# Where attention outputs are turned: from a turn of their own in a ring of banks to the bank of the turned row maxima

## The reference, cut to what matters

```python
xn = layernorm(x)                                   # x: 4 x 512 x 256
q, k, v = xn @ Wq.T, xn @ Wk.T, xn @ Wv.T           # 4 query groups share 8 heads of k and v, 8 wide
scores = einsum('bsqhd,bthd->bqhst', q, k) / sqrt(8)
a_dot  = einsum('bqhst,bthd->bsqhd', softmax(scores), v)
a_mem  = (elu(q) @ memory) / (elu(q) @ memory_norm)
attn   = a_dot * (1 - w) + a_mem * w                # w = sigmoid(memory_weight)
out    = x + attn + moe(xn)                         # 8 experts, top 2, and a shared expert
```

## Time and profile before

| what | value |
|---|---|
| median of 3 runs | 738.71 us (737.17 to 740.52) |
| profiled execution | 736.45 us, of which the span of the instructions is 734.4 us |
| granted TensorE clock, mean | 1.000 |
| busy share of the span | PE 97%, DVE 80%, ACT 67%, POOL 19% |

### The profile page before, as it was taken

How to read it: one execution, slowest core, us unless ns; L and a number is a source line. 1 busy time by engine, 2 the same in 40 slices (tenths; PEclk the granted TensorE clock), 3 DMA queues, 4 the chain that set the end, 5 groups by cost and what they waited for, 6 DMA issues and landing times.

```text
span 734.4 us, 16848 instructions
## 1 busy us (share of the span) xinstructions
PE 712.1 (97%) x5018; PEld 393.1 (54%) x5019; DVE 589.8 (80%) x1040; ACT 490.0 (67%) x886; POOL 137.7 (19%) x298
## 2 busy tenths in 40 slices
PE   8999999899999999999999999899999999999998
PEld 3455544632222222222222223588888888888887
DVE  6276489899999999999999992577777878766755
ACT  2473600299999999999999898756566665656322
POOL 1000000566642222111222211100000000005750
PEclk9999999999999999999999999999999999999999
DMA  9829200168521111001111362051111111122431
GB/s 304 286 71 325 66 1 0 34 204 258 171 64 33 33 34 34 26 25 33 33 33 33 97 223 84 15 172 43 57 50 50 50 50 57 43 101 80 137 109 42
DMA packets 50003, 65.42 MB, mean 89 GB/s; under 512 B 8216, under 2 KB 42928, under 8 KB 49968
## 3 DMA queue, kind: packets, MB, share of 16 engines
q1 hardware_dynamic: 37232, 39.92, 17.2%
q10 hardware_dynamic: 9664, 16.66, 6.9%
q0 software_dynamic: 3072, 8.39, 3.6%
HBM read 40.15 MB, written 24.38 MB: 88 GB/s over the span
## 4 chain that ended last, share of the span: by engine, by line
PE 71%; DVE 12%; issue 8%; ACT 7%; DVEq 1%; POOL 1%; ACTq 1%; POOLq 0%
PE ps L1432 14%; DVE smax L1026 10%; PE ps L1500 9%; PE ps L1401 9%; PE ps L1280 7%; PE ps L1456 7%; PE ps L1534 6%; ACT att L752 5%; PE ps L1272 4%; PE ps L1549 3%; PE ps L1304 3%; PE ps L1491 2%; PE ps L1238 2%; ACT o_sb L711 1%; PE ps L1386 1%
## 5 line engine op out<-in xcount | busy, mean ns | idle before, releaser
L1026 DVE TENSOR_REDUCE smax<-ps 128x1 f32<-128x512 f32 x512 | 309.3, 675 | 8.6 <-PE ps L1304 8.6
L752 ACT ACTIVATE att<-ps 128x512 f32<-128x512 f32 x512 | 273.5, 597 | 34.0 <-PE ps L1456 27.9
L1401 PE MATMUL ps<-att,v_head 128*32 128x256 f32 x2048 | 163.4, 391 | 6.3 <-ACT o_sb L711 5.8
L1456 PE MATMUL ps<-att 51*128 51x512 bf16 x512 | 159.8, 383 | 3.4 <-ACT att L752 1.1
L1304 PE MATMUL ps<-att 48*128 48x512 bf16 x512 | 159.0, 384 | 0.0
L1432 PE MATMUL ps<-att_r 128*128 128x512 f32 x456 | 117.6, 407 | 3.2 <-DVE att_r L1087 3.2
L1083 DVE TENSOR_TENSOR att_r<-big,att_r 128x1024 fp32r<-128x1024 f32 x76 | 89.8, 1222 | 24.7 <-ACT att_r L732 24.6
L1456 PEld LDWEIGHTS ps<-att 51*128 51x128 bf16 x512 | 38.3, 93 | 113.9 <-DVE smax L1026 64.5
L1432 PEld LDWEIGHTS ps<-att_r 128*128 128x128 f32 x456 | 85.6, 188 | 21.8 <-DVE att_r L1087 3.8
L1401 PEld LDWEIGHTS ps<-att,v_head 128*32 128x32 f32 x2048 | 40.6, 108 | 92.5 <-issue 49.3
L732 ACT ACTIVATE att_r<-big 128x1024 fp32r x74 | 74.3, 1052 | 19.4 <-issue 19.3
(11 more groups left out here) (167 smaller groups left out, 702.0 us busy)
## 6 DMA issues: line engine op xcount, KB each, us to landing
big<-w ACTq DMA_DIRECT2D x8, 1024.0 KB
q_stacks<-big SPq DMA_DIRECT2D x12, 512.0 KB
att<-q_stacks SPq DMA_DIRECT2D x64, 96.0 KB
slot_x<-zeros SPq DMA_DIRECT2D x1, 4992.0 KB, 17.9
e_x<-slot_x SPq DMA_DIRECT2D x39, 128.0 KB, 2.0
slot_y<-xn SPq DMA_DIRECT2D x39, 128.0 KB, 1.7
big<-w ACTq DMA_DIRECT2D x8, 512.0 KB
att<-k_stacks SPq DMA_DIRECT2D x64, 48.0 KB
```

Source lines behind the costliest of these rows:

```text
L752: act.activation(probs[:, t % 2, g, :], ps[:, RING[turn_of(u) % 3], :], ACT.Exp, scale=SCALE)\
L1026: dve.reduce_max(smax[:, s % 2, 8 * half + v:8 * half + v + 1], ps[:, bank + half, :], X_AXIS)\
L1401: last = pe.matmul(ps[32 * g:32 * (g + 1), 6, queries], v_head[:, s % 2, t, :], probs[:, t % 2, g, queries], start=s % 2 == 0 and t == 0 a ...
L1456: pe.matmul(ps[:, RING[turn % 3], :], k_st[s][rows, P * t:P * (t + 1)], q_st[s][rows, g, :], start=True, stop=True).then_inc(scores_ready, 1)
```

## The change

Outputs have no turn of their own any more: `turn_of` skips turn 6 alone, the sixteen scores use turns 0 to 5 and 7 to 16, and turn 17 stays empty (`NO_TURN`), so that a step still has 18. The outputs of a pair are now turned in the odd step (the second head) behind the pair, after round 2, just ahead of the turned maxima and in the same bank: maxima in columns 0 to 127, outputs in columns 128 to 415. The transposes become four plain fp32 matmuls of the output against `held`, the 4 by 18 columns of the identity that pick out what is needed. `copy_oT` stands on ScalarE between `negate_max` and exponential 6 of the odd step; `finish_o` stands ahead of the maxima of round 5 of the odd step; `add_o` follows in the next even step. Turn 9 (score 8) waits for both readers of the bank.

```diff
-        TURNS, MAX_AT, OUT_AT = 18, 6, 13
+        TURNS, MAX_AT, NO_TURN = 18, 6, 17
+        OUT_COLS = 2 * (DH + 1)
...
-            return u + (u >= MAX_AT) + (u >= OUT_AT - 1)
+            return u + (u >= MAX_AT)
...
-                    if s == 1 and not first:
-                        add_o(blk * 2 - 1, 1, b if h0 == 4 else b - 1, (h0 - 2) % H)
-                    if s == 3:
-                        add_o(blk * 2, 0, b, h0)
+                    if s % 2 == 0 and not first:
+                        add_o(blk * 2 + (s // 2 - 2), s // 2, b if h0 == 4 else b - 1, (h0 + s - 4) % H)
...
+            add_o(PAIRS - 2, 0, BATCH - 1, H - 4)
             add_o(PAIRS - 1, 1, BATCH - 1, H - 2)
...
-                act.activation(oT_sb[:, a, :, :].rearrange("p (w two) n -> p w (two n)", two=2),
-                               ps[:, bank, :].rearrange("p (w n) -> p w n", n=32)[:, :, 0:2 * (DH + 1)],
-                               ACT.Copy).then_inc(oT_copied, 1)
+                act.activation(oT_sb[:, a, :, :].rearrange("p w n -> p (w n)"),
+                               ps[:, bank, P:P + ST * G * OUT_COLS], ACT.Copy).then_inc(oT_copied, 1)
...
-                    if s % 2 == 0 and not first:
-                        if u == 4:
-                            evacuate_o(blk * 2 + (s // 2 - 1), (s // 2 + 1) % 2)
-                        if u == 12:
-                            copy_oT(blk * 2 + (s // 2 - 1), (s // 2 + 1) % 2)
+                    if u == MAX_AT and s % 2 == 1 and not first:
+                        copy_oT(blk * 2 + (s // 2 - 1), (s // 2 + 1) % 2)
+                    if u == 4 and s % 2 == 0 and not first:
+                        evacuate_o(blk * 2 + (s // 2 - 1), (s // 2 + 1) % 2)
...
-                    if v == 7 and s % 2 == 0 and not first:
+                    if v == 5 and s % 2 == 1 and not first:
                         finish_o(blk * 2 + (s // 2 - 1), (s // 2 + 1) % 2)
...
+                if back == NO_TURN:
+                    return
                 if back == MAX_AT:
-                    wait(pe, negm_ready, i + 2)
-                elif back == OUT_AT:
                     wait(pe, oT_copied, outputs)
+                    if not last:
+                        wait(pe, negm_ready, i + 2)
                 else:
-                    v = back - (back > MAX_AT) - (back > OUT_AT)
+                    v = back - (back > MAX_AT)
                     wait(pe, probs_ready, i * 16 + (v + 1))
...
+            held = ident[:, :].rearrange("p (g n) -> p g n", g=G)[:, :, 0:OUT_COLS]
...
                 for st in range(ST):
-                    last = pe.transpose(ps[:, bank, P * st:P * (st + 1)],
-                                        o_sb[:, a, P * st:P * (st + 1)], ident[:, :])
+                    first = P + G * OUT_COLS * st
+                    last = pe.matmul(ps[:, bank, first:first + G * OUT_COLS], o_sb[:, a, P * st:P * (st + 1)], held,
+                                     start=True, stop=True)
...
-                        if t == OUT_AT // G - 1 and g == PAIR - 1 and s % 2 == 0 and not first:
-                            transpose_o(pair - 1, (s // 2 + 1) % 2)
...
-                        if v == MAX_AT // 2 - 1 and not last:
-                            transpose_max(i + 1, s + 1)
+                        if v == MAX_AT // 2 - 1:
+                            if s % 2 == 1 and not (isinstance(pair, int) and pair == 0):
+                                transpose_o(pair - 1, (s // 2 + 1) % 2)
+                            if not last:
+                                transpose_max(i + 1, s + 1)
```

More of the change, by code:

```diff
@@ L711, in evacuate_o, with copy_oT @@
                 act.activation(o_sb[:, a, :], ps[:, 6, :], ACT.Copy).then_inc(o_copied, 1)
-            def copy_oT(pair, a, bank=RING[OUT_AT % 3]):
+            def copy_oT(pair, a, bank=RING[MAX_AT % 3]):
                 act.wait_ge(oT_in_psum, pair + 1)
                 wait(act, o_ready, pair - 1)
-                act.activation(oT_sb[:, a, :, :].rearrange("p (w two) n -> p w (two n)", two=2),
-                               ps[:, bank, :].rearrange("p (w n) -> p w n", n=32)[:, :, 0:2 * (DH + 1)],
-                               ACT.Copy).then_inc(oT_copied, 1)
+                act.activation(oT_sb[:, a, :, :].rearrange("p w n -> p (w n)"),
+                               ps[:, bank, P:P + ST * G * OUT_COLS], ACT.Copy).then_inc(oT_copied, 1)
             def copy_ex(j, a):
@@ L762, in _ @@
             for i in range(4):
-                exps(0, i, first=i == 0)
+                exps(0, i, first=i < 2)
                 if i == 0:
@@ L1105, in _ @@
             for i in range(4):
-                step(0, i, first=i == 0)
+                step(0, i, first=i < 2)
             with dve.Fori(1, NLOOP - 1) as blk:
@@ L1338, in _, with bank_free @@
             shared_group(1)
-            def bank_free(i, turn, outputs=0):
+            def bank_free(i, turn, outputs=0, last=False):
                 back = turn - 3
@@ L1379, in _, with transpose_o @@
             pe.wait_ge(ones_rows, 128)
-            def transpose_o(pair, a, bank=RING[OUT_AT % 3]):
+            held = ident[:, :].rearrange("p (g n) -> p g n", g=G)[:, :, 0:OUT_COLS]
+            def transpose_o(pair, a, bank=RING[MAX_AT % 3]):
                 pe.wait_ge(o_copied, pair + 1)
                 if not (isinstance(pair, int) and pair == PAIRS - 1):
-                    bank_free(pair * 2 + 2, OUT_AT)
+                    bank_free(pair * 2 + 3, MAX_AT)
                 for st in range(ST):
-                    last = pe.transpose(ps[:, bank, P * st:P * (st + 1)],
-                                        o_sb[:, a, P * st:P * (st + 1)], ident[:, :])
+                    first = P + G * OUT_COLS * st
+                    last = pe.matmul(ps[:, bank, first:first + G * OUT_COLS], o_sb[:, a, P * st:P * (st + 1)], held,
+                                     start=True, stop=True)
                 last.then_inc(oT_in_psum, 1)
@@ L1447, in step @@
                             rows = slice(HALF * half, HALF * half + RM)
-                            if not (last and turn - 3 == MAX_AT):
-                                bank_free(i, turn, pair if s % 2 == 0 else 0)
+                            bank_free(i, turn, pair if s % 2 == 1 else 0, last)
                             if ahead:
```

## The result

The changed kernel takes 748.0 us (median of 4 runs, 747.24 to 749.12) against 738.24 us before, a ratio of 1.0128 with a 95% interval of 1.0108 to 1.0148: some 9.5 us slower by the ratio (9.8 between the medians), clear of the 0.5%. The forecast was 749.0, in a range of 739 to 755, and slower. The profiled execution took 747.24 us, of which the span is 745.1, at a mean granted clock of 1.000 as before.

A forecast was written before the change was run, and what follows sets the result against it. The prediction took TensorE's own rounds to bound the kernel. Its terms summed to +0.83 us a pair, +11.6 over fourteen pairs, +11.2 with the ends, forecasting 749 us in a range of 739 to 755.

The forecast's parts named there:

- The bound: Inside the attention, TensorE's own rounds explain the whole period, 19.64 us a pair; VectorE's own work takes 19.41.
- Rival B: VectorE is the bound and its lead at round 2, odd step, hides the change: -2.9 us, 736; chance 0.10.
- transposes out of round 5, even step: On TensorE, round 5 of the even step loses its four transposes: -0.58 us a pair.
- four fp32 matmuls: In round 2 of the odd step, eight records at 0.128 us each: +1.02 us a pair, lower bound 0.57.
- hole, from rounds 5 and 6 to two boundaries: Empty turn moves from 13 to 17; scores 0 and 1 wait for exponentials two before: -0.31 + 0.62 us a pair.
- round 3, odd step: The matmuls in round 2 let ScalarE catch up, so round 3 loses its stall: -0.15 us a pair.
- copy ahead of exponential 6: ScalarE's copy delays exponentials 6 and 7, so weighted values of round 4, odd step, stall: +0.23 us a pair.
- rival A: The matmuls are cheap, 0.57 us, with no stall in round 4: +0.15 us a pair, 740.5 us; chance 0.15.
- The sign that I gave: In the profile after, rounds 0 would take 1.4 us in both steps.
- The start: At the start TensorE's lead over VectorE, some 0.6 us, is still to be spent: 0.6 us taken off.
- The +0.2 at the end: The fifteenth pair's turn moves from step 30 to 31, where ScalarE hides part of it: +0.2 us.
- rival C: GpSimd becomes late: the split behind `add_o` holds up the turned maxima, 0.5 us a pair, 756 us; chance 0.05.

The follow-up runs named there:

- the version with both edits: Changed kernel with true transposes at the new place and one empty turn in four steps: 736.17 us against 738.11 before, ratio 0.9973.
- the last run above: The version with both edits, with VectorE's reciprocal made three times (twice into a spare tile): 740.97 us against 738.11 before, ratio 1.0044.
- the second copy: Changed kernel with ScalarE's copy of the 288 columns made twice, ahead of exponential 6 of the odd step: 752.73 us against 737.84 before, ratio 1.0188.

## Why the prediction was right, step by step

**The bound.** That TensorE's rounds make the period, and not VectorE, was the step on which all rested. It held: what was added on TensorE's path came out as time and work added on VectorE didn't. In the version with both edits, where VectorE has 0.12 us to spare, 0.30 of the 0.42 added on VectorE came out; work added on TensorE was not tried there. Rival B, for which the chain of waits spoke, is out. It would have needed TensorE under VectorE's 19.34 us a pair.

Of the two grounds that I gave, the sum of the rounds is none, since round starts always add up to the period. The other, that TensorE comes to a score for maxima after the bank is free, I read at one place, with 0.7 us. It holds at every place: over one pair the least distance from the end of the fourth maximum before to the score is 0.26 us before (at 283.00) and 0.44 after (at 263.69). In the last run above, where VectorE does hold TensorE, it is 0.06.

**The terms**, in us a pair:

| term | predicted | after |
|---|---|---|
| transposes out of round 5, even step | -0.58 | round 5 at 1.11: -0.58 |
| four fp32 matmuls | +1.02 | 278.08 to 279.13: +1.05 |
| hole, from rounds 5 and 6 to two boundaries | -0.31 + 0.62 | -0.31 + 0.31 + 0.31 |
| round 3, odd step | -0.15 | round 3 at 1.10: -0.15 |
| copy ahead of exponential 6 | +0.23 | round 4 at 1.23: +0.12 |
| sum | +0.83 | +0.75 (period: +0.76, by the means +0.74) |

The matmuls' price did not go with the columns; rival A is out. That 1.02 came so near is in part luck. The 0.128 was the mean over a row with longer gaps in it (0.21 at its start, 0.14 and 0.22 in its middle); elsewhere in it, as inside the eight, records stand 0.112 apart (last section). Eight of 0.112 make 0.90, and the rest of the 1.05 lies at the ends of the block, which my sum left out: the second record stands 0.17 behind the first, and the turned maxima 0.20 behind the last. The transposes' 0.58 has the same ends, so that 0.45 of the difference is four records more. The Trainium skill's rule on weight loads (TensorE: Matmul & The Clock Gate, LDWEIGHTS) gave an estimate of 0.85 for the eight; the trace has 1.05. A record's 0.112 is near that rule's 0.107; the ends are not in it. The Trainium skill's advice to turn with a transpose (Perfetto Trace Analysis, Transposes) the runs bear out, by 0.45 to 0.47 us a pair at either place.

**The hole** cost its 0.31 at both boundaries. The sign that I gave, rounds 0 at 1.4 in both steps, holds in the odd step (1.37); in the even step half of it lies in the round ahead (1.26 and 1.27).

**The copy's stall** was half of what I said. Exponential 7 ends 281.01 - 279.13 = 1.88 us behind the start of the turned maxima, where I had 1.91, but the weighted values follow it by 0.05, not by the 0.13 that I carried over from the ring's scores. The 1.88 is itself met by luck: negating starts at +0.35, no sooner than before, where I took +0.27, but the copy follows it by 0.17 (279.48 to 279.65), where I took 0.24. The mechanism is shown by the second copy, which cost its whole 0.29.

**The start.** I took 0.6 off for a lead of TensorE that would first be used up. There is none to see: by the turned maxima the changed kernel is behind by 0.35 us in step 1, 1.11 in step 3, where the first outputs are turned, 1.80 in step 5 and 2.53 in step 7, so that the first pair costs as much as the later ones. It contradicted my own first step, since an engine that no one holds has no lead to give back; its extra work counts from the first pair. The +0.2 at the end is not seen either (291.8 and 291.7). These two and the copy's stall cancelled in part: 11.2 predicted on the span's own terms, 10.7 measured, of which 0.4, ahead of the attention, belongs to no step of the prediction.

**Hidden, as said:** GpSimd's additions and VectorE's reciprocal in the last step. The turned maxima follow the outputs directly (279.13) and nothing waits for GpSimd there, so rival C is out.

## What to carry to other kernels

When three engines look full, take one engine's rounds and ask what lengthens each of them: where none waits for the other engine, that other one is not the bound, and a little work added to it tells for certain. A delay that is taken out of a place may have been the cover of another stall; ask what now stands bare. And where a turn in a ring is given up, see whether the ring got shorter: an empty turn makes the next two scores wait for the reader two before them, just as a used one does (0.31 us here, where nothing hid it), and one in four steps did what one in each step did.

## What the runs showed that I had not expected

A plain fp32 matmul with 128 by 128 weights is two records that stand 0.112 us apart, whether 72 or 130 columns go through it, and a 128 by 128 fp32 transpose is one record, 0.110 behind the one before. So the form cost what its four additional records cost. The rows are of parts of a block, without its first record: the eight of the changed kernel, then from the kernel before four transposes and the row.

```profile
278.25 0.94 PE L1393 MATMUL ps<-ident,o_sb 128*128 128x72 f32 x7
```

```profile
287.48 0.49 PE L1386 MATMUL ps<-ident,o_sb 128*128 128x128 f32 x3
141.60 0.83 PE L1373 MATMUL ps<-mem_w,big 128*128 128x130 f32 x6
```

Their records are 0.274, 0.273 and 0.275 long, so the distances are 0.67 / 6, 0.22 / 2 and 0.56 / 5. The weight loads of the eight start 0.111 apart too. That the loads set the distance fits this and was not tried by itself.

What follows a finished exponential on TensorE starts 0.14 us behind it for a score (274.84 to 274.98) and 0.05 behind it for weighted values (281.01 to 281.06). The cause of the difference stays open.
